# Two of 48 gathered tiles moved from an indirect DMA to single-row DMAs in a graph network kernel

## What is computed

```python
h = jnp.maximum(_layernorm(x, axis=-1), 0.0)
h = h @ enc_w + enc_b
h_list = [h]
for l in range(3):
    e = edge_attr @ edge_w[l] + edge_b[l]
    msg = relu(h_list[l][src] + e)
    agg = segment_sum(msg, dst, num_segments=n_nodes)
    z = (1.0 + eps[l]) * h_list[l] + agg
    z = relu(z @ mlp_w1[l] + mlp_b1[l]) @ mlp_w2[l] + mlp_b2[l]
    h_list.append(relu(z))
out = x + (concatenate(h_list, axis=1) @ out_w + out_b)
```

## Time and profile before

| | us |
|---|---|
| median of three runs | 7461.86 (7454.96 to 7464.24) |
| the profiled execution | 7395.73 |
| its span, first to last instruction | 7393.9 |
| first window of layer 0 | about 185 |
| TensorE's granted clock, mean share of 2.4 GHz | 0.558 |

### The profile page before, as it was taken

One profiled execution on the slowest core, in us unless ns is written; L12 is line 12 of the kernel. 1 busy time (PEld: TensorE's weight loads), 2 busy tenths in 40 slices (PEclk: granted clock), 3 DMA queues, 4 the chain that ended last, 5 costly groups with the idle time before them and its releaser, 6 DMA issues.

```text
span 7393.9 us, 56283 instructions
## 1 busy us (share of the span) xinstructions
PE 4774.5 (65%) x14396; PEld 3131.3 (42%) x14397; DVE 1663.8 (23%) x4168; ACT 999.7 (14%) x1597; POOL 4751.3 (64%) x5075
## 2 busy tenths in 40 slices
PE   5666666666666646666666666673666666666667
PEld 4444444444444424444444444442444444444444
DVE  4222222222222212222222222221222222222222
ACT  4111111111111101111111111110111111111111
POOL 5666666666666466666666666646666666666664
PEclk7555555555555555555555555555555555555555
DMA  3122212222222112222222222211111111111112
GB/s 116 53 54 54 55 53 54 54 55 54 54 54 54 44 49 54 55 55 54 54 55 55 53 54 56 55 43 51 51 51 52 51 52 51 52 51 51 52 52 72
DMA packets 191126, 404.82 MB, mean 55 GB/s; under 512 B 85159, under 2 KB 87927, under 8 KB 190439
## 3 DMA queue, kind: packets, MB, share of 16 engines
q0 software_dynamic: 159456, 326.88, 17.0%
q1 hardware_dynamic: 21759, 56.75, 2.6%
q10 hardware_dynamic: 9840, 20.48, 0.8%
HBM read 378.08 MB, written 25.69 MB: 55 GB/s over the span
## 4 chain that ended last, share of the span: by engine, by line
another core or an unknown queue 44%; PE 27%; issue 18%; DVE 6%; DVEq 3%; ACT 3%; POOL 0%; DMA 0%; ACTq 0%
PE bank L624 14%; PE bank L620 9%; DVE rows L879 3%; ACT rows L543 2%; DVE onehot L865 2%; PE bank L651 1%; PE bank L664 1%; PE bank L643 1%; DVEq L939 1%; DVE agg_t L875 1%; PE bank L645 1%; DVEq L247 1%; DVEq L875 0%; PE bank L661 0%
## 5 line engine op out<-in xcount | busy, mean ns | idle before, releaser
L372 POOL DMA_INDIRECT rows<-h_table,idx x4983 | 4714.0, 946 | 2575.5 <-issue 1417.7
L624 PEld LDWEIGHTS bank<-onehot,rows 128*128 128x128 f32 x9966 | 2178.6, 310 | 3367.3 <-ACT rows L543 1966.2
L624 PE MATMUL bank<-onehot,rows 128*128 128x64 f32 x9966 | 2158.1, 394 | 2162.8 <-ACT rows L543 1599.7
L620 PE MATMUL bank<-edgew,attr 65*128 65x512 f32 x2496 | 2279.0, 1026 | 9.6 <-DMA w2s<-w 9.6
L543 ACT ACTIVATE rows<-rows 128x512 f32<-128x512 f32 x1248 | 783.1, 628 | 5381.1 <-DVE rows L879 4213.0
L875 DVE TENSOR_TENSOR agg_t<-bank,agg_t 128x64 f32 x1248 | 278.1, 223 | 4790.4 <-remote 3542.9
L879 DVE TENSOR_TENSOR rows<-bank,rows 128x512 f32<-128x512 f32 x1248 | 857.6, 687 | 83.2 <-DMA rows<-h_table,idx 35.2
L620 PEld LDWEIGHTS bank<-edgew,attr 65*128 65x128 f32 x2496 | 677.7, 316 | 280.6 <-issue 280.6
L865 DVE TENSOR_TENSOR onehot<-bank,dst_rel 128x256 f32<-128x256 f32 x1248 | 518.3, 415 | 205.4 <-issue 205.4
L651 PE MATMUL bank<-hid,w2s 128*128 128x512 f32 x300 | 195.3, 769 | 192.5 <-ACT hid L506 124.8
L664 PE MATMUL bank<-outw,h_t 128*128 128x128 f32 x588 | 151.7, 423 | 62.0 <-ACT h_t L515 58.5
(11 more groups left out here) (83 smaller groups left out, 478.6 us busy)
## 6 DMA issues: line engine op xcount, KB each, us to landing
rows<-h_table,idx POOLq DMA_INDIRECT x4983
attr<-ea_t SPq DMA_DIRECT2D x156, 256.0 KB
h_table<-h_n ACTq DMA_DIRECT2D x48, 256.0 KB
h_table<-rows SPq DMA_DIRECT2D x24, 256.0 KB, 2.1
out<-out_acc SPq DMA_DIRECT2D x24, 256.0 KB
out_acc<-x_t ACTq DMA_DIRECT2D x4, 1280.0 KB, 11.5
rows<-dst_g SPq DMA_DIRECT2D x1, 832.0 KB
rows<-dst_t SPq DMA_DIRECT2D x1, 832.0 KB
```

The costliest lines, as they stand in the source:

```text
L372: return g.indirect_dma_start(dst, None, h_table[l % 2], bass.IndirectOffsetOnAxis(ap=index, axis=0))
L620: return nc.tensor.matmul(dst[0:EP, 0:tiles * D], cols, edgew[:, l, 0:tiles * D], start=True, stop=True)
L624: last = nc.tensor.matmul(dst[:, 0:WIN], rows[0:EP, slot, j, :], onehot[0:EP, hot_slot, j, :], start=(j == 0), stop=(j == tiles - 1))
```

## The change

The ring has 12 groups now (`RING = 12`, two halves of 6; the `rows` tensor keeps 16 slots, `SLOTS`, of which 12 are used). A round loop thus runs 34 full rounds and a rest of 8 groups a layer. In groups 5 and 11 of each full round GpSimd gathers three tiles; the fourth comes by 128 plain DMAs of one 512-byte row each, 64 issued by SyncE and 64 by ScalarE. Each reads 32 byte offsets at a time from a small table `row_at` in SBUF into registers (made once from a new input `src_g` and a multiplication on VectorE). All 128 count semaphore `fetched`, for which VectorE waits besides `gathered`.

ScalarE no longer takes relus in the edge loop: VectorE writes rows plus edge terms into the PSUM bank and takes the relu from there into the rows. The node units' relus are VectorE's too, and a unit's `node_out` and `node_take` come at kk = 4 and kk = 5. ScalarE's loop holds the stores (of the last layer's output as well) and its half of the row DMAs; SyncE's holds attribute loads and the other half.

```diff
-HB = 8
-RING = 16
+HALVES = ((0, 6), (6, 6))
+HB = 6
+RING = 12
+SLOTS = 16
+ROW_GROUPS = (5, 11)
+BY_SYNC = 64
+CHUNKS = (32, 32)
...
+        def fetch_rows(eng, l, b, u, first, chunks, named):
+            for count in chunks:
+                with ExitStack() as held:
+                    at = [held.enter_context(eng.register(f"row_at{next(named)}")) for _ in range(count)]
+                    eng.load(at, row_at[u:u + 1, bass.ds(b * EP + first, count)])
+                    for i in range(count):
+                        row = rows[first + i:first + i + 1, ROW_GROUPS[u], TG - 1, :]
+                        eng.dma_start(row.bitcast(u8), table_row(l, eng, at[i])).then_inc(fetched[u], 16)
+                first += count
...
+                    for u, group in enumerate(ROW_GROUPS):
+                        if not isinstance(b, int):
+                            start, n = HALVES[u]
+                            wait_apart(sp, e_done, b * RING + (l * NG + start + n + S0 - RING))
+                            load_attr(b * RING + start, u, n)
...
+                        freed(group)
+                        fetch_rows(sp, l, b, u, 0, CHUNKS, named)
...
+                with nc.Fori(0, NFULL - 1, engines=(mybir.EngineType.Activation,), hint_back_edge=True) as c:
+                    for half, (start, n) in enumerate(HALVES):
+                        store_unit(c, half)
+                        wait_apart(act, agg_done, c * RING + (l * NG + ROW_GROUPS[half] + 1 + S0))
+                        fetch_rows(act, l, c + 1, half, BY_SYNC, CHUNKS, named)
...
+                        part = rows[0:EP, k, 0:tiles, :]
+                        total = e_ps[k % NE_PS][0:EP, 0:tiles * D].rearrange("p (t d) -> p t d", d=D)
+                        v.tensor_tensor(total, total, part, ALU.add).then_inc(summed, 1)
+                        dve.wait_ge(summed, first_group + (k + 1 + S0))
+                        v.tensor_scalar(part, total, 0.0, None, ALU.max).then_inc(relued, 1)
+                        if kk in (2, 3, 5) and in_full:
                             with dve.If(unit > 0):
-                                node_take(unit_before(unit))
+                                (relu_z if kk == 2 else relu_h if kk == 3 else node_take)(unit_before(unit))
```

More of the change, by code:

```diff
@@ L43, in gnn_kernel @@
     NGP = NTE // TG
-    NB = NGP // HB
-    NBU = NG // HB
+    NB = NGP // RING * 2
+    NBU = NFULL * 2 + sum(REST >= start + n for start, n in HALVES)
     L = w1.shape[0]
@@ new lines, in _ @@
+                if l == 0:
+                    for u in range(4):
+                        sp.wait_ge(p_stored[u], (NI + 3 - u) // 4 * 16)
+                    sp.wait_ge(row_at_bytes, 1)
+                else:
+                    sp.wait_ge(stored, l * NU * 16 + 16)
+                fetch_body(0)
+                with nc.Fori(1, NFULL, engines=(mybir.EngineType.SP,), hint_back_edge=True) as b:
+                    fetch_body(b)
+                for half, (start, n) in enumerate(HALVES):
+                    sp.wait_ge(e_done, (NFULL - 1) * RING + l * NG + start + n + S0)
+                    load_attr(NFULL * RING + start, half, min(n, REST - start))
@@ L331, in _ @@
+                for half, (start, n) in enumerate(HALVES):
+                    if l < L - 1:
+                        sp.wait_ge(e_done, NFULL * RING + l * NG + min(start + n, REST) + S0)
+                        load_attr(start, half, n)
                 far_passes(sp, load_extra(sp), far_pass)
[L332 to L335, removed]
@@ L399, in _ @@
                     tiles = min(TG, NTR - group * TG)
-                    if tiles < TG:
+                    if slot in ROW_GROUPS and group < NFULL * RING:
+                        tiles = TG - 1
+                    elif tiles < TG:
                         g.inc_swdge_sem([gathered[slot]], [16 * (TG - tiles)], mode="add")
@@ L527, in store_last @@
                        .then_inc(stored, 16)
[L529 to L546, removed]
@@ L548, in _, with store_unit @@
-                with nc.Fori(0, NFULL, engines=(mybir.EngineType.Activation,), hint_back_edge=True) as b:
-                    edge_body(b, RING)
-                edge_body(NFULL, REST)
+                def store_unit(b, half):
+                    unit = load_unit(act, b * 2 + half)
+                    with act.If(unit > 0):
+                        (store if l < L - 1 else store_out)(unit_before(unit))
+                act.wait_ge(stored, l * NU * 16 + 16)
+                for u in range(2):
+                    fetch_rows(act, l, 0, u, BY_SYNC, CHUNKS, named)
@@ L691, in edge_body @@
                     for k in range(groups):
[L692 to L693 removed]
+                        half, kk = in_half(k)
+                        in_full = groups >= sum(HALVES[half])
+                        if kk == 0 and in_full:
                             unit = load_unit(pe, b * 2 + half)
```

172 lines of the change are left out of this document (109 added, 63 removed).

## The result

On the chip of the prediction the changed kernel takes 9248.9 us (median of four runs, 9234.41 to 9258.69) against 7463.05 us of the kernel before: 1.239 times as long, interval 1.238 to 1.241. The forecast was 7,231 us.

The account below looks back on a forecast made before the run. Bound: GpSimd's gathers at 1.25 us plus waits for slots while TensorE's reports stall. Terms: gathers -255, ring -41, round ends +40, units +25, in all -231, giving 7231 us as a median; range 7,130 to 7,500.

Parts of the forecast that it names:

- The bound: Edge loop: GpSimd's issue time at 1.25 us a gather plus a wait for every 13.7 gathers, while TensorE's reports stall.
- the price of a row DMA: SyncE's and ScalarE's loops: issuing one row costs c = 0.3 to 0.41 us, so SyncE's round fits in 67.2 us, costing nothing.
- The part on row DMAs: SyncE's and ScalarE's queues: 128 issues each a round fit; a fetch takes under 35 us and has nearly a round.
- Ring: Layer ends: 12 groups instead of 16 to walk through after the last gather, -41 us.
- round ends: TensorE has no edge terms made ahead at 27 more places; +40 us taken, bounds 0 and +92.
- relus: Edge loop and node units: relus moved to VectorE are hidden by TensorE's 3.41 us a group; 0, bounds -60 and +60.
- units: Node units' three relus on VectorE stand ahead of the next window add; +25 us taken, bounds 0 and +153.
- The gathers' -255 us: 204 gathers leave GpSimd at 1.25 us each, counted in full; bounds 0 and -255 us.
- B: Rival: SyncE becomes the bound through issuing row DMAs at c = 0.52 us, about 8,410 us; 16%.
- A: Rival: GpSimd's waits grow by what the gathers save, TensorE's reports being the pace; about 7,480 to 7,540 us; 12%.
- C: Rival: row DMAs hold up TensorE's reports too, doubling some 340 waits, near 8,280 us; 6%.
- D: Rival: reports stall after a number of gathers, not a time, so some 5% fewer waits, about 7,150 us; 6%.

## Why the prediction was wrong, step by step

**The bound.** The cycle of gathers, late reports and pauses was read rightly as a pattern, but as to what sets its length the text took GpSimd's 1.25 us plus a wait. The run with memsets shows the loop to keep 1.43 us a gather (5.7 us a group) with either pace of GpSimd, and its pauses to be what is left over.

**The step that failed: the price of a row DMA.** "I take c = 0.3 to 0.41, since both nearest rows are single rows." Both stand in the prologue. SyncE's issue at 40.66 us comes before GpSimd's first gather at 58.00. ScalarE's at 76.32 and 76.57 do not:

```profile
75.70 0.95 POOL L372 DMA_INDIRECT rows<-h_table,idx  x1 [0.30 <-issue]
76.96 0.95 POOL L372 DMA_INDIRECT rows<-h_table,idx  x1 [0.30 <-issue]
```

GpSimd had then gathered for 18 us without a pause, and these few issues were quick all the same; why, no run shows. In loops such a stretch is slow: beyond 10 us into one, none of ScalarE's 224 intervals in the changed kernel is under 0.4 us. Without gathers, and on the faster kind, the term is right (0.32 us on average within a batch). With gathers on the slower kind it is 0.61, beyond the 0.449 from which the prediction had the kernel slower. By the prediction's own formula the round is then 128 x 0.61 + 12 = 90 us, where 87.5 were measured on average and 67.2 assumed. So the other part of the formula, 12 us for loads, attributes and steps, was about right, although a load of 32 registers took 2.04 us in the median and not 1.6.

**The row that said so.** It was among those cited, and was used for the opposite: "near the end SyncE issued 22 output stores in 27.01 us". The first of these stores were issued while GpSimd still gathered, the others behind its last gather at 7339.65. The line's instructions in the two stretches, 7,326 to 7,341 us and 7,342 to 7,356 (count, min/median/max in ns):

```profile
L334 SPq MOVE out<-out_acc x6: 7/19/697, 7327.2 to 7337.4; - x6
L334 SPq DMA_DIRECT2D out<-out_acc x6: 3/14/351, 7327.9 to 7338.1; - x6
...
L334 SPq MOVE out<-out_acc x15: 29/29/29, 7342.5 to 7355.1; - x15
L334 SPq DMA_DIRECT2D out<-out_acc x15: 338/339/339, 7342.6 to 7355.2; - x15
```

In the second stretch a store starts every 0.90 us, steadily; that is what a pass of this loop takes. In the first, stores start 0.9 to 4.3 us apart, and a register move takes up to 0.697 us instead of 0.029. The prediction had found that reports of one engine wait while GpSimd gathers, and didn't ask whether the queues of SyncE and ScalarE do the same.

**Attributes behind rows.** The part on row DMAs says that a fetch "has nearly a round from the freeing of its slot to its use". That holds for the rows; the attribute load behind them has less. It is 3816.4 us of waiting in the run with SyncE's unused rows.

**The other terms.** Ring, round ends, relus and units together had +24 us; measured -27 (0.996 of 7395.7) on the slower kind. Relus and units are 0 on the faster kind (1.0003), where +25 was taken. The gathers' -255 us show where they are the bound: 6,342 to 6,097 us on the faster kind, -246, from the kernel with 64 unused rows of ScalarE to the changed one in the same job. The prediction's whole sum was -231 us, and the change measured -227 there. That agreement is in part luck, since the +25 in it was nothing and the terms of the ring weren't measured one by one; on the chip of the prediction the sum never came to count.

**Rivals.** B is what happened: SyncE without waits and the chain in its queue. It had 16% and a point value of 8,410 us by c = 0.52. A, waits that grow by what the gathers save, stays open: no run took gathers away and put no rows in their place. The run with memsets speaks for it, since there GpSimd's pauses shrank by what its work grew. C, rows that hold up reports, has at most 1.4% in the run with half the rows and 2.7% in the third layer of the one with ScalarE's 128; what was found works the other way round, from the gathers to the rows. D isn't seen.

The Trainium skill's rule in "DMA: Bandwidth & Descriptors", section "Rules for kernel authors", to coalesce small transfers, pointed the right way on the slower kind; on the faster one the change gained 3.6% with its 26,112 single-row DMAs. The fixed 2.0 us, which the Trainium skill gives in the same page's section "Anatomy of one DMA — SWDGE (gpsimd) path" for DMAs that GpSimd issues, and puts down mostly to completion, are no issue cost here. SyncE's and ScalarE's rows cost 0.31 and 0.32 us to issue without gathers, though on the slower kind, over 10 us into a run of gathers, it is 2.1 us on average.

No version beat before by much on both kinds: without rows it is 0.996 on the slower one; the change itself is 0.964 on the faster and 1.24 on the slower; one tile with split rows 0.983 and 1.021.

## What to carry to other kernels

Take the price of an instruction from a loop that runs beside the same neighbours, and not from a few single ones: an issue of 0.31 us was 0.61 on average beside GpSimd's gathers, and 2.1 when they had gone on for over 10 us, while a few quick ones in the prologue had stood beside gathers too. When a queue gets much new work, list what stands behind it (here attribute loads and unit stores), since that can be late where the new work is not. And measure on more than one chip: the sign of this change differed between them.

## What was unexpected of the hardware

- Two kinds of chip, or of its state: the kernel before takes 7,393 to 7,464 us in five of seven jobs and 6,322 to 6,323 in two, with GpSimd's gather at 0.95 us on both.
- On the slower kind the loop keeps one gather in 1.43 us. Data land in time, but VectorE waits up to 26.1 us for a report of TensorE, and SyncE's and ScalarE's rows start 1.4, 2.1 or 2.8 us apart when GpSimd has long been gathering, 4.2 us at most.
- More work on GpSimd, 0.083 us a gather, is free there (0.9963 against 0.9962), and the longest wait for a report is 18.3 us instead of 26.1.
- A plain DMA of one row costs its issuing engine 0.313 us (SyncE) or 0.322 us (ScalarE) where no gathers run, and a load of 32 registers takes SyncE 2.04 us in the median.
